# Attention's value products in full float32, in two halves of TensorE's columns

## The reference

```python
x = x + 0.5 * _L0_ffn_ref(_layernorm(x), ...)      # 2 shared units + top-2 of 8 experts
x = x + _L0_attn_ref(_layernorm(x), Wq, Wk, Wv, Wo)
x = x + 0.5 * _L0_ffn_ref(_layernorm(x), ...)

# _L0_attn_ref as it is fed here: b = 2, s = 1024, 16 query heads, 4 key heads, head width 32
q, k = rope(x @ Wq.T), rope(x @ Wk.T); v = x @ Wv.T   # keys and values repeated 4 times
scores = einsum('bhqd,bhkd->bhqk', q, k) * 32 ** -0.5
attn = softmax(scores, axis=-1)
out = einsum('bhqk,bhkd->bhqd', attn, v)
return out @ Wo.T
```

## Time and profile before

| | us |
|---|---|
| three executions | 1725.16, 1726.25, 1728.23 |
| median | 1726.25 |
| the profiled execution | 1731.96 |
| span in the profile | 1730.2 |
| PE busy | 1636.0 (95%) |
| DVE busy | 1022.8 (59%) |
| POOL busy | 974.8 (56%) |
| ACT busy | 838.8 (48%) |

### The profile page before, as it was taken

How to read it: one execution, slowest core, us unless ns; L and a number is a source line. 1 busy time by engine, 2 the same in 40 slices (tenths; PEclk the granted TensorE clock), 3 DMA queues, 4 the chain that set the end, 5 groups by cost and what they waited for, 6 DMA issues and landing times.

```text
span 1730.2 us, 24272 instructions
## 1 busy us (share of the span) xinstructions
PE 1636.0 (95%) x8164; PEld 1289.3 (75%) x8164; DVE 1022.8 (59%) x1738; ACT 838.8 (48%) x1172; POOL 974.8 (56%) x736
## 2 busy tenths in 40 slices
PE   6998999999998889999999999999999999999997
PEld 5776889998877666666666666656777889999985
DVE  5553322222277789999999999976655422222236
ACT  4421322222323239999999999893542223233320
POOL 3106286405558658888878888861222447632645
PEclk9999999999998889999999999999999999999998
DMA  8306355324262230110010000003101544533327
GB/s 331 117 18 230 140 183 182 126 85 172 103 196 78 81 74 20 32 25 20 19 35 23 20 19 20 7 19 149 55 1 63 190 156 172 184 126 127 135 87 241
DMA packets 67843, 175.69 MB, mean 102 GB/s; under 512 B 10768, under 2 KB 11664, under 8 KB 65424
## 3 DMA queue, kind: packets, MB, share of 16 engines
q1 hardware_dynamic: 54896, 100.48, 17.8%
q0 software_dynamic: 12832, 73.67, 11.9%
HBM read 102.29 MB, written 55.84 MB: 91 GB/s over the span
## 4 chain that ended last, share of the span: by engine, by line
PE 55%; DVE 25%; DMA 7%; issue 6%; ACT 4%; POOL 1%; SPq 1%; another core or an unknown queue 0%; DVEq 0%; ACTq 0%; POOLq 0%
PE PS L1152 10%; PE PS L1154 9%; PE PS L1153 9%; DVE nmf_later L1953 6%; DVE Pl L1980 4%; DVE nmf_first L1953 4%; DMA xn<-x_routed 4%; DVE Ph L1972 3%; DMA xs<-x_routed 2%; PE PS L1289 2%; PE PS L1294 2%; PE PS L1292 2%; PE PS L1291 2%; PE PS L1293 2%; PE PS L1290 2%
## 5 line engine op out<-in xcount | busy, mean ns | idle before, releaser
L2129 POOL TENSOR_TENSOR Pl<-PT,Ph 128x1024 fp32r<-128x1024 f32 x162 | 420.2, 2611 | 103.0 <-ACT Ph L1654 72.7
L1645 ACT ACTIVATE PT<-PS 128x1024 f32<-128x1024 f32 x256 | 259.0, 1014 | 27.9 <-PE PS L1384 27.5
L1654 ACT ACTIVATE Ph<-PT 128x1024 fp32r<-128x1024 f32 x198 | 209.3, 1057 | 3.6
L1404 PE MATMUL PS<-Ph,V 128*65 128x512 f32 x496 | 200.3, 404 | 0.4 <-ACT OT L1662 0.4
L1406 PE MATMUL PS<-Pl,V 128*65 128x512 f32 x496 | 195.9, 395 | 0.0
L1953 DVE TENSOR_REDUCE nmf_later<-PS 128x1 f32<-128x1024 f32 x160 | 188.8, 1211 | 10.7 <-PE PS L1365 10.7
L2029 POOL TENSOR_TENSOR W<-raw,W 128x544 fp32r<-128x544 f32 x144 | 190.3, 1355 | 1.5
L1384 PE MATMUL PS<-QS,KS 98*128 98x512 f32 x512 | 176.0, 427 | 13.5 <-DVE nmf_later L1953 9.8
L1920 DVE TENSOR_TENSOR thid<-thid,PS 128x352 f32<-128x352 f32 x78 | 40.7, 522 | 247.3 <-ACT thid L1578 247.3
L1365 PE MATMUL PS<-KS,QS 96*128 96x512 f32 x512 | 165.8, 406 | 7.6 <-ACT PT L1645 2.4
L1578 ACT ACTIVATE thid<-PS 128x352 f32<-128x352 f32 x78 | 36.3, 466 | 262.3 <-PE PS L1294 262.3
(11 more groups left out here) (197 smaller groups left out, 3985.9 us busy)
## 6 DMA issues: line engine op xcount, KB each, us to landing
raw<-ffn_w POOLq DMA_DIRECT2D x18, 2176.0 KB, 10.3
y_routed<-ytile SPq DMA_DIRECT2D x78, 256.0 KB, 2.0
xn<-x_routed SPq DMA_DIRECT2D x40, 256.0 KB, 2.9
x_routed<-xq SPq DMA_DIRECT2D x1, 9984.0 KB, 29.4
xs<-x_routed SPq DMA_DIRECT2D x38, 256.0 KB, 3.0
QS<-later_hi SPq DMA_DIRECT2D x112, 64.0 KB, 2.0
raw<-ffn_w SPq DMA_DIRECT2D x6, 768.0 KB, 10.9
raw<-ffn_w SPq DMA_DIRECT2D x16, 272.0 KB
```

Source lines behind the costliest of these rows:

```text
L1404: e.matmul(PS[0:VCOL, ob, :], V[:, b * QT + kt, g, :], high_part(u)[:, js], start=kt == 0, stop=False)
L1645: e.activation(PT[:, u % PTBUF, :], PS[:, i:i + 2, :].rearrange("p b n -> p (b n)"), ACT.Exp, scale=SCALE).then_inc(p_ready.sem, 1)
L1654: e.activation(high_part(u)[:], PT[:, u % PTBUF, :], ACT.Copy).then_inc(ph_act.sem, 1)
L2129: e.tensor_tensor(low_part(u)[:], PT[:, u % PTBUF, :], high_part(u)[:], ALU.subtract).then_inc(pl_pool.sem, 1)
```

## The change

`PT` goes to TensorE as it is, with both operands in float32, for every unit. `V` has 33 columns: values and ones. The matmul of a unit's even key tile writes partitions 0 to 32 of the sum's bank, that of the odd tile partitions 64 to 96, so each lies in one half of the array's 128 columns (`COLS = 64`; tile sizes 128x64 at columns 0 and 64). The two sums are added on DVE after the transpose. `Ph`, `Pl`, `split_hi`, `split_lo` and the buffers of both are gone, and so is the lo part of `V`.

The order is written anew: the values come 2 units after their scores (`LAG`); in the third unit of a half none stand, in the fourth two units' values in a row. `store_head` stands in the third unit. An exponential waits now until the values of the unit four before have read its `PT` buffer. In the projections, ACT's copy of a value tile no longer waits for the queries of the eighth tile, and the bank is free when the keys have been rotated.

```diff
-VCOL = 2 * HD + 1
-PTBUF, PHBUF, PLBUF = 4, 6, 5
-LAG, FULL_LAG = 5, 3
+VCOL = HD + 1
+COLS = P // 2
+PTBUF = 4
+LAG = 2
...
 def ends_half(u):
-    return in_full(u + 1) if u % 4 == 2 else u % 4 == 3 and not in_full(u)
+    return u % (QT // 2) == QT // 2 - 1
...
-        in_parts = u > 0 and not in_full(u - 1)
-        if in_parts:
-            work.append(("split_hi", u - 1))
-            if not lo_on_vector(u - 1):
-                work.append(("split_lo", u - 1))
         work.append(("scores", u))
...
-        w = u - LAG if u >= LAG and not in_full(u - LAG) else None
+        due = {2: [], 3: [u - LAG - 1, u - LAG]}.get(pair, [u - LAG])
+        for w in due if u >= LAG else ():
+            work.append(("values", w))
+        if outputs and pair == 2:
+            work.append(("store_head", *outputs.pop(0)))
+        outputs.extend(unit(w)[:3] for w in due if u >= LAG and ends_half(w))
         if n + 1 < groups:
             work.append(("row_max", n + 1, un // QT, un % QT))
...
-        if n + 2 < groups and un % (UNITS // 2) == 6:
+        if n + 2 < groups and un % (UNITS // 2) == 8:
             work.append(("turn_queries", n + 2, un // (UNITS // 2)))
...
-                free[bkv] = (v_lo, t)
+                free[bkv] = (k_products, t)
...
-        def values(u, *tiles):
+        def values(u):
...
-                    e.matmul(PS[0:VCOL, ob, :], V[:, b * QT + kt, g, :], high_part(u)[:, js],
-                             start=kt == 0, stop=False)
-                    mm = e.matmul(PS[0:VCOL, ob, :], V[:, b * QT + kt, g, :], low_part(u)[:, js],
-                                  start=False, stop=end)
+            for j in range(2):
+                mm = e.matmul(PS[j * COLS:j * COLS + VCOL, ob, :], V[:, b * QT + 2 * pair + j, g, :],
+                              PT[:, u % PTBUF, j * GRP:(j + 1) * GRP], start=pair == 0, stop=ends_half(u))
...
-                mm = e.transpose(PS[:, MISC, j * VCOL:(j + 1) * VCOL], OT[0:VCOL, j * P:(j + 1) * P],
-                                 identf[0:VCOL, 0:VCOL])
+                mm = e.transpose(PS[:, MISC, j * P:j * P + COLS + VCOL], OT[0:COLS + VCOL, j * P:(j + 1) * P],
+                                 identf[0:COLS + VCOL, 0:COLS + VCOL])
...
-                    if is_projected_after(t, QT):
-                        act.wait_ge(q_ready, PROJECTED[QT - 1])
...
-                if u >= PTBUF and in_full(u - PTBUF):
+                if u >= PTBUF:
                     act.wait_ge(pv_done, u - PTBUF)
-                elif u >= PTBUF:
-                    parts_ready(act, u - PTBUF)
...
-            dve.step(e.reciprocal(rL[:, q, :], o[:, :, HD]))
-            dve.step(e.tensor_copy(head[:, q, :, :], o[:, :, HD + 1:]))
-            dve.after_step()
-            dve.step(e.tensor_tensor(o[:, :, 0:HD], head[:, q, :, :], o[:, :, 0:HD], ALU.add))
+            e.tensor_reduce(head[:, q, :, :], o, AX.X, ALU.add).then_inc(halves_summed.sem, 1)
+            dve.wait_ge(halves_summed, n, h, hf)
+            dve.step(e.reciprocal(rL[:, q, :], head[:, q, :, HD]))
```

More of the change, by code:

```diff
@@ L465, in order_of_work @@
             maxima.append((n + 1, un // QT))
[L466 to L475, removed]
-        if n + 2 < groups and un % (UNITS // 2) == 6:
+        if n + 2 < groups and un % (UNITS // 2) == 8:
             work.append(("turn_queries", n + 2, un // (UNITS // 2)))
-        if n + 2 < groups and un % (UNITS // 2) == 7:
+        if n + 2 < groups and un % (UNITS // 2) == 9:
             work.append(("place_queries", n + 2, un // (UNITS // 2)))
@@ L482, in order_of_work @@
     end = groups * UNITS
-    assert in_full(end - 1) and LAG > FULL_LAG
-    for w in [v for v in range(end - LAG, end - 2) if not in_full(v)] + [end - 1, end - 2]:
+    for w in range(end - LAG, end):
         work.append(("values", w))
[L486 to L489, removed]
+    work.append(("store_head", *unit(end - 1)[:3]))
     work.append(("attention_end",))
@@ L639, in macaron @@
     rL, at = place("rL", (P, 2, TPG), F32, at)
[L640 to L647, removed]
+    head, at = place("head", (P, 2, TPG, VCOL), F32, at)
     nmf_later, at = place("nmf_later", (P, 2 * REP, QT), F32, at)
     assert at <= wqkv_at + 2 * DC * QKV * 4
-    parts = [place(f"Ph{i}", (P, 2 * GRP), F32R, parts_at[i])[0] for i in range(PHBUF)]
-    parts += [place(f"Pl{i}", (P, 2 * GRP), F32R, parts_at[PHBUF + i])[0] for i in range(PLBUF)]
     PS = ctx.enter_context(nc.psum_tensor("PS", [P, 8, GRP], F32))
@@ L881, in macaron @@
             p_ready.plan(*key)
[L882 to L886, removed]
+        elif kind == "values":
             u = key[0]
@@ L891, in macaron @@
         elif kind == "store_head":
-            for a in (ot_turned, head_ready):
+            for a in (ot_turned, halves_summed, head_ready):
                 a.plan(*key)
@@ L999, in macaron @@
     ends = [tuple(unit(key[0])[:3]) for kind, *key in work
-            if kind in VALUES and is_whole(key) and ends_half(key[0])]
+            if kind == "values" and ends_half(key[0])]
     end_place = {key: i for i, key in enumerate(ends)}
@@ L1392, in values @@
             ob = out_bank(n, hf)
-            parts_ready(pe, u)
-            if pair == 0 and 0 in tiles:
+            pe.wait_ge(p_ready, u)
+            if pair == 0:
                 until_free(ob)
[L1396 to L1401, removed]
-                                  start=False, stop=end)
-                else:
-                    e.matmul(PS[0:VCOL, ob, :], V[:, b * QT + kt, g, :], high_part(u)[:, js],
-                             start=kt == 0, stop=False)
-                    mm = e.matmul(PS[0:VCOL, ob, :], V[:, b * QT + kt, g, :], low_part(u)[:, js],
[L1407 to L1410, removed]
+            for j in range(2):
+                mm = e.matmul(PS[j * COLS:j * COLS + VCOL, ob, :], V[:, b * QT + 2 * pair + j, g, :],
+                              PT[:, u % PTBUF, j * GRP:(j + 1) * GRP], start=pair == 0, stop=ends_half(u))
+            mm.then_inc(pv_done.sem, 1)
+            free[ob] = (ot_ready, n, h, hf)
         def store_head(n, h, hf):
@@ L1482, in tensor_program @@
             elif kind == "values":
-                values(*key, 0, 1)
-            elif kind == "half_values":
                 values(*key)
```

96 lines of the change are left out of this document (19 added, 77 removed).

## The result

The changed kernel takes 1761.49 us (median of 4 runs, 1759.44 to 1769.86), the kernel before, beside it, 1725.70 (4 runs, 1724.89 to 1728.23). The ratio is 1.0214, 95% interval 1.0179 to 1.0249: slower, by about 2%. The forecast was 1747, by case (C).

The account below looks back on a forecast made before the run. DVE sets the pace before, with PE 10% behind; after the change TensorE does. By (C), 1732 + 26 (seven groups) - 4 (last group) - 1 (projections) = 1753, less 5.7 to the median: 1747 us, range 1730 to 1800.

Parts of the forecast that it names:

- (C): Values on TensorE: passes leave in program order, 11 passes or 4.72 us a half; 1747 us, chance 0.46.
- (D): Rival: a 0.19 us pause at each change between whole and halved array, on top of (C); 1820 us, chance 0.07.
- (B): Rival: even and odd tile wholly beside each other, 8 passes of time or 3.43 us a half; 1665 us, chance 0.20.
- (E): Rival between (B) and (C): odd tile's first pass begins before the even's second, or less wait; about 1700, chance 0.10.
- The longer transposes: Transposes of 97 rows instead of 65, costed at nothing, between 0 and half of their 0.22 us a half.
- The fourth unit's wait: Scores of a half's fourth unit wait for the second unit's maxima: estimated 0.3 us a half, between 0 and 0.8.
- PE waits nowhere but in a half's fourth unit: Sign in the seven groups' profile after: TensorE's only wait is there, for a maximum.
- the exponential's covered wait: The exponential's new wait, for values of the unit four before, is covered: they precede its own scores on TensorE.
- the reduction at 425 ns: At a half's end on DVE: reducing 264 sums to 132 takes 425 ns like an earlier one, +23 us.
- the last group: The group without maxima, 60.2 us to the end of its values before, was forecast at 56.4, so -4.
- The projections: ACT no longer waits for the eighth queries and DVE loses 16 short subtractions: -1 us, between 0 and -3.
- (A): Rival: the halves don't work at once, 16 passes or 6.86 us a half; 1886 us, chance 0.17.

Follow-up runs that it names:

- The even-first order: The changed kernel with both even key tiles before both odd ones in a run of two units: 1766.56 us, ratio 1.0228.
- the experiment: The changed kernel with the split of the turned queries on ACT and DVE, and their DMAs, one unit earlier: 1740.55 us, ratio 1.0088.

## Why the prediction came out near, and where it was wrong

**The step that failed** is the choice of (C): "the queue keeps its order". It was taken from rows in which four passes are evenly 0.43 apart, but those were matmuls of one and the same part of the array; no row of before had a free half. Passes pair up across halves, so the values take 8 pass times, 3.43 us for the 4.72 of the sum. The even-first order shows that it holds even past a waiting matmul.

**The second error hid the first**, so that the number came near is luck. (D)'s pause, which stood there only on top of (C) and with a chance of 0.07, is real: 3 x 0.32 = 0.96 us a half. Values and pauses make 4.39 for 4.72. What the prediction had as rivals came together: (B)'s passes, in the order of starts that (E) names, and (D)'s pauses. The longer transposes, costed at nothing, take 0.28 up to the next matmul instead of 0.22. Left out was 0.08 that the first matmul behind transposes loses, here twice, since the maxima are transposed in this half too; the kernel before shows it as well (in the earlier trace rows, two score matmuls take 0.55 behind transposes and not 0.465). The fourth unit's wait was right: 0.19, and 0.10 for a weight load that it lays open, for the 0.3 of the estimate. So a half is 8.86 (902.21 to 911.10, less 0.03 for the transposed maxima) where 8.96 was forecast, from other terms: 3.72 for scores and maxima, 3.43, 0.96, 0.28, 2 x 0.08, 0.29, and 0.02 that I can't place.

**The wait that was not seen** makes the difference to 1761. "PE waits nowhere but in a half's fourth unit" is wrong: the change moves the queries' lo part from the eighth to the tenth of 16 units and the transposes from the second to the third unit of a half, and both now meet at one bank. With the clock that falls behind some of them, these waits cost 22 us, by the experiment; without them the kernel takes 1740.55, 6 under the forecast. The list of work showed both moves; I counted the transposes' number and not the bank's last reader.

**Right** were the bound (TensorE, with DVE at 62% and ACT at 52%, forecast about 60% and half), the exponential's covered wait (of ACT's 202.0 us idle before exponentials, 201.5 are for scores), the reduction at 425 ns as in the earlier trace rows, the last group (4.1 us less from its first exponential to its last eviction, 1156.22 to 1212.23, forecast 4), and that it is slower. The projections gave 2 to 4 us, for 1. **(A)** is refuted by the kernel with both tiles in one half, at 1990. **(B)** had the overlap. With the pauses in it, it would have been 1665 + 64 x 0.96 = 1726, and with 22 for the lo part 1748: 13 short, of which the longer transposes and the 0.08 make some 11 (64 x 0.14 + 28 x 0.08).

## What to carry to other kernels

When a stage is handed to the engine that waits least, price the new work at its borders too: a matmul that changes how the array is divided pays at entry and exit, so the number of runs counts, not only the number of matmuls. Before an instruction is moved, list who last read the bank that it writes, and where that reader stands in its own engine's queue. And test a saving with its neighbours in place: the work that was taken from between two bank users was also the time in which the banks came free.

## What the runs showed of the hardware

- Full float32 matmuls in two halves of the columns start 6 ns apart and take together what one takes alone (0.429 us a pass of 512 columns); with one more matmul between them in the program, 13 ns apart. Side by side a float32 matmul costs 0.43, near the 0.465 of the hi and lo products.
- Going from 128-column fp32r matmuls to 64-column halves and back costs 0.32 us a round by starts, and 0.31 by the difference of two kernels at a clock of 1.00. The Trainium skill's page "TensorEngine Tiling (Array Packing)", in "Key Properties", says that a change of mode drains TensorE; the price seen here agrees with that. Going to 66 columns of the whole array and back costs nothing (2.64 for a sum of 2.65).
- Behind the same idle time of 1.54 us, the granted clock stayed at 1.00 in one group and fell in another (from 844 to 848 it is 0.57, part at each of the two levels, 1.2 and 2.4 GHz), and the first pass of a run and the next in the same half then started 0.85 us apart instead of 0.45. Groups with such a fall are 1.6 us longer (75.9 for 74.4), so a wait of 1.5 us can cost as much again.
